# A two-layer transformer block on one core: small steps of the last layer's quantised product moved between GpSimd, VectorE and ScalarE

## The reference

```
x = x + _L1_xattn_ref(_layernorm(x, axis=-1), ctx_1024, ctx_1024, mask_BxS_bk1)
x = x + _L1_ffn_ref(_layernorm(x, axis=-1), L1_ffn_weight_int8, L1_ffn_weight_scale, L1_ffn_bias)

def _L1_ffn_ref(x, weight_int8, weight_scale, bias):
    x2 = x.reshape(-1, K)
    x_scale = jnp.maximum(jnp.abs(x2).max() / 127.0, EPS)
    x_int8 = jnp.clip(jnp.round(x2 / x_scale), -128, 127).astype(jnp.int8)
    acc_i32 = jax.lax.dot_general(x_int8, weight_int8.T, ...)
    out = acc_i32.astype(jnp.float32) * x_scale * weight_scale.T
    out = out + bias
```

## Time and profile before

| | |
|---|---|
| median of 3 runs | 918.49 us |
| the profiled execution | 917.72 us |
| its span, first to last instruction | 916.0 us |
| TensorE busy | 894.1 us, 98% |
| VectorE busy | 595.5 us, 65% |
| ScalarE busy | 537.8 us, 59% |
| GpSimd busy | 262.3 us, 29% |

### The profile page before, as it was taken

One profiled execution on the slowest core, in us unless ns is written; L12 is line 12 of the kernel. 1 busy time (PEld: TensorE's weight loads), 2 busy tenths in 40 slices (PEclk: granted clock), 3 DMA queues, 4 the chain that ended last, 5 costly groups with the idle time before them and its releaser, 6 DMA issues.

```text
span 916.0 us, 19720 instructions
## 1 busy us (share of the span) xinstructions
PE 894.1 (98%) x6719; PEld 788.9 (86%) x6719; DVE 595.5 (65%) x1603; ACT 537.8 (59%) x1285; POOL 262.3 (29%) x354
## 2 busy tenths in 40 slices
PE   5999999999999999999999999999999999999997
PEld 4888888998888898888898888987898999998776
DVE  6678766666666666665666666666764666438767
ACT  4666555555565556555565565666572455356875
POOL 1344234324343343342343343244100000023200
PEclk9999999999999999999999999999999999999999
DMA  9313000000000000000000000000252043355522
GB/s 278 104 41 110 1 19 22 7 17 5 17 5 22 17 5 17 5 22 17 5 17 5 17 13 13 1 6 7 100 184 87 1 132 130 110 140 178 167 69 81
DMA packets 29501, 50.24 MB, mean 55 GB/s; under 512 B 2960, under 2 KB 24112, under 8 KB 27680
## 3 DMA queue, kind: packets, MB, share of 16 engines
q1 hardware_dynamic: 27920, 45.97, 16.1%
q0 software_dynamic: 1536, 3.67, 1.4%
HBM read 41.37 MB, written 8.26 MB: 54 GB/s over the span
## 4 chain that ended last, share of the span: by engine, by line
PE 93%; DVE 5%; ACT 1%; issue 1%; DMA 1%; POOL 0%; DVEq 0%
PE bank L1871 28%; PE bank L1900 10%; PE bank L2116 9%; PE bank L2028 9%; PE bank L1919 9%; PE bank L1885 8%; PE bank L1940 5%; PE bank L1844 4%; PE bank L2203 2%; PE bank L2221 2%; PE bank L1853 1%; PE bank L2080 1%; PE bank L1817 1%; PE bank L2210 1%; DVE neg_max L1300 1%
## 5 line engine op out<-in xcount | busy, mean ns | idle before, releaser
L773 POOL TENSOR_TENSOR probs<-probs,row_rcp 112x375 f32<-112x375 f32 x256 | 209.2, 840 | 389.6 <-DVE row_rcp L1306 388.2
L899 ACT ACTIVATE probs<-bank,neg_max 112x375 f32<-112x375 f32 x256 | 144.2, 569 | 55.0 <-DVE neg_max L1300 54.7
L1900 PE MATMUL bank<-ident,probs 112*125 112x112 f32 x768 | 129.1, 278 | 1.8 <-DVE probs_t L1311 1.8
L1300 DVE TENSOR_REDUCE neg_max<-bank 112x1 f32<-112x375 f32 x256 | 123.3, 539 | 10.3 <-PE bank L1885 10.1
L1900 PEld LDWEIGHTS bank<-ident,probs 112*125 112x125 f32 x768 | 113.5, 187 | 18.6 <-issue 3.7
L1311 DVE COPY probs_t<-bank 125x336 f32<-125x336 f32 x128 | 64.7, 506 | 60.7 <-PE bank L1900 56.7
L871 ACT ACTIVATE k_parts<-bank 128x376 fp32r<-128x376 f32 x128 | 62.0, 485 | 67.6 <-PE bank L1871 67.6
L1871 PE MATMUL bank<-ctx_hi,down_hi 128*128 128x376 f32 x256 | 96.8, 378 | 0.6 <-DVE k_parts L1291 0.3
L874 ACT ACTIVATE v<-bank 125x512 f32<-125x512 f32 x96 | 57.5, 599 | 63.5 <-PE bank L1871 63.5
L1291 DVE TENSOR_TENSOR k_parts<-bank,k_parts 128x376 fp32r<-128x376 f32 x128 | 69.8, 546 | 29.9 <-ACT k_parts L871 28.8
L1919 PEld LDWEIGHTS bank<-probs_t,v 125*64 125x64 f32 x1536 | 74.0, 137 | 16.2 <-issue 16.0
(11 more groups left out here) (239 smaller groups left out, 1994.6 us busy)
## 6 DMA issues: line engine op xcount, KB each, us to landing
ctx_raw<-in_ctx_t SPq DMA_DIRECT2D x16, 375.0 KB, 3.4
stage<-in_ffn_up SPq DMA_DIRECT2D x5, 1024.0 KB, 5.0
stage<-in_ffn_down SPq DMA_DIRECT2D x5, 1024.0 KB, 6.9
ring_late<-in_ctx_t SPq DMA_DIRECT2D x10, 375.0 KB, 10.2
ring_late<-in_ctx_n SPq DMA_DIRECT2D x10, 375.0 KB
routed<-xn SPq DMA_DIRECT2D x1, 2240.0 KB, 9.5
rows_in<-routed SPq DMA_DIRECT2D x5, 448.0 KB, 6.3
answers<-y_rows SPq DMA_DIRECT2D x10, 224.0 KB, 2.7
```

Source lines behind the costliest of these rows:

```text
L773: eng.tensor_tensor(probs[s][:, :], probs[s][:, :], row_rcp[:, s:s + 1].broadcast_to([S, C]), ALU.mult).then_inc(probs_ready, 1)
L899: eng.activation(probs[r][:, :], SCORE_BANKS[i][0:S, 0:C], ACT.Exp, bias=neg_max[:, r:r + 1], accum_out=row_sum[:, r:r + 1]).then_inc(exp_ ...
L1300: eng.tensor_reduce(neg_max[:, r:r + 1], SCORE_BANKS[k][0:S, 0:C], AX.X, ALU.max, negate=True) \
L1900: t = eng.transpose(turn_bank(i, project)[0:CJ, j * S:(j + 1) * S], probs[QUAD * v + i][:, j * CJ:(j + 1) * CJ], ident[0:S, 0:S])
```

## The change

Four things are edited.

1. The outputs' scale is made by VectorE, behind the rounding of group 1 and ahead of its next scaling, and no longer by GpSimd.
2. The turned integers of group 3 are copied by VectorE, between its additions for groups 0 and 1, and no longer by ScalarE. TensorE's products of group 3 wait for this copy through a semaphore of its own.
3. ScalarE centres batch 15 too.
4. ScalarE's first square roots (and the table load) stand behind its centring of batch 11, ahead of those of batches 12 to 15; its second roots stand behind the centring of batch 15.

```
-            eng.wait_ge(late_loaded, 16 * 3)
-            eng.wait_ge(scale_step, 4)
-            eng.tensor_scalar(out_scale[:, :], ws_col[:, :], x_scale[:, 0:1], None, ALU.mult) \
-               .then_inc(out_scale_ready, 1)
...
-            attn_out(B - 1)
-            for t in range(B - 5, B - 1):
-                centre(t)
-            eng.wait_ge(abs_zeroed, 2)
-            for cols in (slice(0, B - 4), slice(B - 4, B)):
+            def last_root(cols):
...
+            attn_out(B - 1)
+            centre(B - 5)
+            eng.wait_ge(abs_zeroed, 2)
+            last_root(slice(0, B - 4))
+            for t in range(B - 4, B):
+                centre(t)
+            last_root(slice(B - 4, B))
...
             answers_out(1)
-            xi_out(NG - 1)
             answers_out(NG - 2)
...
-            eng.wait_ge(extreme_step, B - CENTRED)
-            eng.wait_ge(norm4.step, 2 * B)
-            eng.tensor_scalar(centred[(B - 1) % CENTRED], x_all[:, B - 1, :], norm4.moments[:, B - 1, 0:1], None,
-                              ALU.subtract).then_inc(last_centred, 1)
             largest_rest(B - 3)
             largest_rest(B - 2)
-            eng.wait_ge(last_centred, 1)
             largest_rest(B - 1)
...
                 quantise(i)
+                if i == 1:
+                    eng.tensor_scalar(out_scale[:, :], ws_col[:, :], x_scale[:, 0:1], None, ALU.mult) \
+                       .then_inc(out_scale_ready, 1)
                 if i + 2 < NG:
                     own_ratios(i + 2)
-            for i in range(NG):
+            add_answers(0)
+
+            eng.wait_ge(xi_turned, NG)
+            eng.wait_ge(acc_ready, KT * (NG - 2))
+            eng.tensor_copy(xi_t[(NG - 1) % 2][:, :, :], bank_b[(NG - 1) % 2][:, 0:KT * GT]
+                            .rearrange("p (k t) -> p k t", k=KT)).then_inc(last_xi_ready, 1)
+            for i in range(1, NG):
                 add_answers(i)
...
             def products(i):
-                eng.wait_ge(xi_t_ready, i + 1)
+                if i < NG - 1:
+                    eng.wait_ge(xi_t_ready, i + 1)
+                else:
+                    eng.wait_ge(last_xi_ready, 1)
```

More of the change, by code:

```diff
@@ L340, in build_program @@
         centred_ready = sem("centred_ready")
-        last_centred = sem("last_centred")
         root_step = sem("root_step")
@@ L377, in build_program @@
         xi_t_ready = sem("xi_t_ready")
+        last_xi_ready = sem("last_xi_ready")
         acc_ready = sem("acc_ready")
@@ L1676, in largest_rest @@
             def largest_rest(t):
-                if t < B - 1:
-                    eng.wait_ge(centred_ready, t + 1)
+                eng.wait_ge(centred_ready, t + 1)
                 eng.tensor_reduce(extreme[:, t:t + 1], centred[t % CENTRED], AX.X, ALU.max, apply_absolute_value=True) \
```

## The result

The changed kernel is slower: 920.89 us (median of 7 runs, 919.57 to 922.16) against 918.54 us (7 runs, 917.81 to 920.51), a ratio of 1.0022 with a 95% interval of 1.0011 to 1.0032, or 1.0 to 2.9 us. The forecast was 918.2 and no change. The profiled execution took 920.89 us, its span is 918.9 us.

What follows compares the result with a forecast made beforehand. In the last 27 us it took VectorE's chain to the reciprocal, then alternating TensorE turns and VectorE additions, as the bound. -0.4 + 0.12 = -0.28 us made 918.49 into 918.2; own range 917.9 to 918.6, 8-in-10 range 917.7 to 919.2.

Steps and rivals of the forecast that it cites:

- the overlap at the start: Kernel start: GpSimd's code load ahead of the identity would stay hidden, with 0.7 us to spare.
- The sum, -0.4 + 0.12: Changed last section: 0.4 us gained before the reciprocal, 0.12 lost in the tail, -0.28 us in all.
- the last rival: Kernel start: GpSimd's missing code delays the identity, costing time from a 7.5 us load on; visible cost 0.06.
- The slack: Kernel start: 0.7 us to spare before GpSimd's code load would cost time, one to one beyond 7.5 us.
- 924.3 for a doubled load: Kernel start: if input loads doubled GpSimd's code load, the identity comes at 16.0, 6.1 us late: 924.3.
- Centring and roots: Ahead of the reciprocal: ScalarE centres batch 15, table load hidden earlier; 0.4 us gained, bounds 0.2 and 0.45.
- The scale on VectorE: Between reciprocal and third group's integers: VectorE's 128x2 scale adds 0.1 us, bounds 0.05 and 0.24; GpSimd's removal worth nothing.
- drain: Behind ScalarE's table load: the Trainium skill's about 1380 ns on top of 1283 ns; the forecast saw no room for it.
- The copy: Tail: VectorE's copy of group 3 takes 1.08 us, delaying that group's products; 0.12 us lost, scale's 0.1 included.
- ScalarE's freed time: Tail: ScalarE loses a 0.94 us copy, so group 2's outputs could start about 907.2 instead of 907.57; no gain counted.
- everything removed counts: Last section: all removed work, 0.35, about 0.6 and 0.94 us, is saved, 1.9 us: 916.6; chance 0.03.
- The dear table switch: ScalarE's table load in its new place costs twice its row, 919.1; chance 0.16, shared with like small losses.

Runs made afterwards that it cites:

- e7: Changed kernel with SyncE holding back all input loads, first rows of x included, until GpSimd's identity is written; 926.67 us in one run.
- e3: Kernel before with only the last group's copy of turned integers moved to VectorE; 918.42 us against 918.18, ratio 0.9998.
- e4: Kernel before with only batch 15 centred by ScalarE and the first roots earlier; 917.92 us against 918.18, ratio 0.9996.
- e8: Changed kernel with the outputs' scale left on GpSimd; 916.46 us against 917.35 for the kernel before, ratio 0.9993.
- e2: Kernel before with only the outputs' scale moved from GpSimd to VectorE; 920.35 us against 918.18, ratio 1.0029.
- e5: Kernel before with an unread second partition maximum behind the scale as GpSimd's last instruction; 920.11 us against 918.38, ratio 1.0015.
- e1: Changed kernel with an unread 128x2 scaling added as GpSimd's last instruction; 917.22 us against 918.18 for the kernel before, ratio 0.9992.
- e9: Changed kernel with the unread GpSimd scaling at its end, run again; 916.82 us against 917.35 for the kernel before, ratio 0.9995.

## Why the prediction was wrong

**The step that failed** is the overlap at the start. The sum, -0.4 + 0.12, holds no term for GpSimd's missing code, because the last rival said: "So the load would be hidden with 0.7 us to spare." The mechanism, its place, and the instruction that would wait were described rightly there; that it would stay hidden was wrong. I took 6.85 us from a stretch without DMA traffic and kept it for the stretch with the most. There the stall lasts from 1.28 to 11.43, 10.1 us, passes the slack, and TensorE's first work comes some 2.1 us later (below). With a stall of the quiet length the step would have held: in e7 the identity is ready at 8.35 us (8.07 + 0.28), and in the six kernels with an early identity TensorE's first work stands at 9.0 at the earliest. The slack was thin besides: 9.90 is one trace, and the mean of the six is 9.42, which leaves 0.2 us over the 9.2 of the prediction and not 0.7.

The weight was wrong too, 0.06 of the chances. The page for the kernel before shows DMA at 9 tenths in its first slice, and no row priced a stall under such traffic. That left the length open and deserved more than 0.06.

**The size.** The forecast's 924.3 for a doubled load was too high because the load grew by half only. As for the measured loss, TensorE's first work starts at 11.2 to 11.8 us in the three kernels with the late identity (mean 11.55) and at 9.0 to 9.9 in the six others (mean 9.42; what varies there is when the first rows of x land). That is 2.1 us lost, less 0.56 gained: 1.6 us slower, within the measured 1.0 to 2.9. The two profiled executions differ by more, 3.2 us. From TensorE's first work to the filler it is 881.40 us before and 882.47 after, but 882.60 and 882.71 in e3 and e4, whose starts are on time, and 880.53 in e8. So the 1.07 us between the first two aren't evidence of the change. Whether a late start adds to it (882.6 and 883.7 in e2 and e5) stays open.

**Centring and roots: right.** 0.4 forecast, 0.44 measured, in all five kernels that have the edit. The table load cost its row, 1.28 us, and was hidden. No drain behind it was seen: the root starts 0.02 us later, and 0.01 in the trace before.

**The scale on VectorE: right in place, too dear.** 0.1 forecast, 0.01 measured, below my lower bound of 0.05. Its 0.22 us overlap the end of the rounding ahead and the start of the scaling behind. That taking it off GpSimd would be worth nothing to ScalarE is borne out by e2 (0.05 us at most) and e3, whose tail with ScalarE's wait is as short as the changed kernel's without it.

**The copy: the term was mis-sized.** 1.08 us forecast from copies of 32-bit data, 0.62 measured, 896 elements. That is the low bound, the rounding's rate, and what the Trainium skill ("VectorE: DVE Perf Modes", "Why PSUM operands drop a tier") allows for 16-bit data out of PSUM; the trace agrees with it. With 1.08 the copy would have ended at 910.70 (909.62 + 1.08) and held up the products of group 3, which start at 910.67, by about 0.1 us. With 0.62 TensorE reaches them by its own order, 13.56 us behind the reciprocal in both kernels. The prediction named ScalarE's freed time here but put it at nothing: its outputs of group 2 start 12.51 us behind the reciprocal instead of 12.96, the turn of answers 2 follows 0.06 us earlier and the addition behind it 0.11. So the last stretch gives -0.12 us instead of +0.12.

**The other rivals.** That everything removed counts didn't happen; ScalarE's idle times of 0.60, 0.26 and 0.29 us in the tail, which the kernel before doesn't have, are where most of its saved time went. The dear table switch didn't happen either.

## What to carry to other kernels

What an engine runs last can decide how its next execution starts: before taking the last ordinary instruction from GpSimd, look at what kind of instruction it leaves behind, and end the program with the kind that it starts with, by an instruction nobody waits for if need be. A stall's length, read in a quiet stretch, isn't its length where transfers are dense; when a hidden cost has 0.7 us of cover, that difference decides. A chain's share of "issue" is no finding until it is split by time. And a saving of half a microsecond in the last 30 us can be read in a profile, from milestone to milestone, where 11 runs can't tell it from nothing; equal stretches in several traces tell how far to trust it, here 0.06 us.

## What the runs showed of the hardware

- GpSimd's last instruction decides the start of the next execution. With a partition maximum last, the identity comes at 10.27 to 11.43 us (changed kernel, e2, e5); with an ordinary instruction last, at 1.52 (kernel before, e1, e3, e4, e8, e9).
- The switch shows as idle time put down to "issue". Ahead of an ordinary instruction it is 6.8 to 7.6 us without DMA traffic (7.04 in e7, 7.59 in e1), and 9.2 to 10.4 under the input loads, which moved about 280 GB/s in the first 12 us. Ahead of the second maximum of e5 it is 5.90, while the output's stores moved 80 GB/s.
- VectorE copied 896 bf16 elements on 128 partitions out of PSUM in 0.62 us, while 336 elements of fp32 took 0.51.
- A 128x2 scaling on VectorE between two long operations cost 0.01 us of a 0.22 us instruction.
- A table load of ScalarE took 1.28 us, and the root behind it started 0.01 to 0.02 us later.
